# New step orders and PSUM bank assignments for a two-layer cross-attention kernel

## The reference

```python
# layer 0 (the image-token part is empty: 77 tokens, all text)
q, k, v = split(x @ Wq.T), split(text @ Wk.T), split(text @ Wv.T)
x = merge(softmax(q @ k.T / 4) @ v) @ Wo.T + bo + x
# layer 1
probs_t  = softmax(q @ k_t.T / 4)                 # 73 text tokens
text_out = probs_t @ v_t
qsem = l2norm(probs_t @ text_ehs)
fused = q @ k_ip.T / 4 + 0.5 * (qsem @ l2norm(ip_ehs).T)   # 4 image tokens
ip_out = (softmax(fused) * spatial_mask) @ v_ip
x = (text_out + ip_out) @ W_out + b_out + x
```

## Time and profile before

| what | value |
|---|---|
| median of 3 runs | 2372.46 us (2371.49 to 2372.55) |
| profiled execution: its own time / its span | 2372.11 us / 2370.3 us |
| mean granted TensorE clock | 0.984 of full speed, 1.00 from 430 us to 2290 us |
| busy share of the span: PE, DVE, ACT, POOL | 93%, 78%, 72%, 67% |
| DMA engines busy, first stage / second stage | 0.91 to 0.51 / about 0.44 |

### The profile page before, as it was taken

How to read it: one execution, slowest core, us unless ns; L and a number is a source line. 1 busy time by engine, 2 the same in 40 slices (tenths; PEclk the granted TensorE clock), 3 DMA queues, 4 the chain that set the end, 5 groups by cost and what they waited for, 6 DMA issues and landing times.

```text
span 2370.3 us, 86625 instructions
## 1 busy us (share of the span) xinstructions
PE 2200.8 (93%) x32824; PEld 1391.7 (59%) x32824; DVE 1849.0 (78%) x3709; ACT 1707.6 (72%) x2732; POOL 1589.4 (67%) x1056
## 2 busy tenths in 40 slices
PE   7999967999999999999999999999999999999984
PEld 5777744555555555555555555555555555555542
DVE  6856644888888888888888888888888888888873
ACT  4323326788888888888888888888888888888862
POOL 4121225777777777777777777777777777777762
PEclk9999988999999999999999999999999999999997
DMA  9877642444444444444444444444444444444431
GB/s 273 267 230 210 204 132 62 114 121 120 123 119 121 117 121 114 117 121 121 122 122 118 120 121 122 120 123 118 122 120 118 114 116 122 123 120 121 118 93 58
DMA packets 338308, 310.64 MB, mean 131 GB/s; under 512 B 180224, under 2 KB 281856, under 8 KB 337920
## 3 DMA queue, kind: packets, MB, share of 16 engines
q1 hardware_dynamic: 337920, 305.36, 46.1%
HBM read 164.66 MB, written 105.98 MB: 114 GB/s over the span
## 4 chain that ended last, share of the span: by engine, by line
PE 44%; POOL 14%; ACT 13%; issue 8%; DVE 3%; DMA 2%; SPq 1%; ACTq 0%; POOLq 0%; DVEq 0%
PE psum L1013 17%; ACT ef L1211 10%; POOL e L1445 7%; PE psum L1117 7%; PE psum L1099 5%; PE psum L1078 5%; POOL ust L1407 5%; PE psum L1016 3%; POOL al L1412 2%; ACT q_high L1192 2%; PE psum L1082 2%; PE psum L1037 2%; PE psum L1129 2%; DMA rb<-r_dram 1%; PE psum L1052 1%
## 5 line engine op out<-in xcount | busy, mean ns | idle before, releaser
L1445 POOL TENSOR_TENSOR e<-ef,eh 73x1024 f32<-73x1024 f32 x320 | 680.3, 2133 | 201.2 <-PE psum L1129 118.5
L1211 ACT ACTIVATE ef<-psum 73x1024 f32<-73x1024 f32 (+1 forms) x640 | 636.2, 1014 | 72.5 <-PE psum L1082 68.6
L1273 DVE TENSOR_REDUCE mneg<-psum 128x8 f16<-128x616 f32 (+3 forms) x512 | 450.9, 934 | 8.9 <-PE psum L1037 2.3
L1301 DVE TENSOR_TENSOR e<-psum,e 73x1024 f32<-73x1024 f32 x320 | 385.6, 1205 | 10.4 <-PE psum L1117 5.8
L1099 PE MATMUL psum<-ef,values 128*32 128x256 f32 x5120 | 360.1, 386 | 0.5
L1117 PE MATMUL psum<-eh,gram 128*73 128x512 f16 x1280 | 337.7, 386 | 18.7 <-DVE mneg L1273 14.2
L1226 ACT ACTIVATE eh<-ef 73x1024 f16<-73x1024 f32 x320 | 337.4, 1055 | 7.7 <-ACT ef L1211 0.4
L1219 ACT ACTIVATE ust<-psum 128x512 f32<-128x512 f32 x384 | 222.4, 596 | 124.0 <-POOL al L1412 116.2
L1407 POOL TENSOR_TENSOR ust<-ust,rb 128x768 f32<-128x768 f32 x128 | 232.3, 1815 | 104.9 <-DMA rb<-r_dram 104.9
L1412 POOL TENSOR_TENSOR al<-ust,ah 128x768 f16<-128x768 f32 x128 | 210.2, 1642 | 85.5 <-ACT ah L1251 85.5
L1281 DVE SCALAR_TENSOR_TENSOR q_low<-psum,q_high 128x512 f16<-128x512 f32 (+1 forms) x256 | 112.8, 481 | 182.4 <-ACT q_high L1192 182.4
(11 more groups left out here) (188 smaller groups left out, 4815.0 us busy)
## 6 DMA issues: line engine op xcount, KB each, us to landing
rb<-r_dram SPq DMA_DIRECT2D x128, 384.0 KB, 3.8
keys<-k_dram SPq DMA_DIRECT2D x128, 231.0 KB, 4.0
values<-v_dram SPq DMA_DIRECT2D x128, 192.5 KB
ust<-ust SPq DMA_DIRECT2D x512, 48.0 KB, 2.4
v_dram<-vst SPq DMA_DIRECT2D x64, 320.0 KB
out<-outt SPq DMA_DIRECT2D x64, 320.0 KB, 2.3
k_dram<-kst SPq DMA_DIRECT2D x32, 616.0 KB, 4.0
x<-in_x SPq DMA_DIRECT2D x32, 384.0 KB, 5.1
```

Source lines behind the costliest of these rows:

```text
L1211: act.activation(ef[l][0:m, unit_heads(n), :].rearrange("t h s -> t (h s)"), src, ACT.Exp, scale=SM).then_inc(s_exp[l], 1)
L1273: dve.tensor_reduce(dst, o, AX_X, ALU.max, negate=True).then_inc(s_max[l], 1)
L1301: dve.tensor_tensor(rest, banks(l, f"u{k}", 2)[0:m, :, :], rest, ALU.mult).then_inc(s_wr, 1)
L1445: pool.tensor_tensor(e2[0:m, k, :, :], ef[1][0:m, unit_heads(k), :], eh[0:m, unit_heads(k), :], ALU.subtract).then_inc(s_e2, 1)
```

## The change

All five lists of `ORDER` and the bank table `USES` are replaced. No step, no instruction and no transfer is added, removed or resized.

```diff
 ORDER = {
     "pe": """
-        1u2/3 1a1/3 0t1/1 1q0/2 1q1/2 0t2/1 0a0/1 1s0/2 0a1/1 1s1/2 0a2/1 1i/2 1a2/3 1u3/3 1m/2 1u4/3 1t0/2 0q0/0 0q1/0 1n0/3 1n1/3
-        1n2/3 1p/4 1u0/2 1n3/3 1n4/3 0s0/0 1a0/2 0s1/0 1u1/2 1t1/2 1o0/4 1o1/4 1t2/2 0m/0 1y/3 0o0/1 0o1/1 0t0/0""",
+        1q0/2 1q1/2 0t2/1 0a0/1 0a1/1 1s0/2 0a2/1 1s1/2 1u3/3 1a2/3 1i/2 1m/2 1u4/3 1t0/2 0q0/0 1n0/3 1p/4 1n1/3 1n2/3
+        1u0/2 0q1/0 0s0/0 1n3/3 1n4/3 0s1/0 1a0/2 1u1/2 1t1/2 1o0/4 1o1/4 1t2/2 0m/0 0o0/1 0o1/1 1y/3 0t0/0 1u2/2
+        1a1/2 0t1/0""",
     "act": """
-        0t0/1 0t1/1 1h4/3 1a1/3 0t2/1 1f/4 0t3/1 1q0/2 1q1/2 0t4/1 0a0/1 1r/3 0a1/1 0a2/1 1i/2 1a2/3 1m/2 0r/1 1t0/2 1h0/2
-        1t1/2 0q0/0 0q1/0 1h1/2 1g/4 1n/3 1a0/2 0g/1 1t2/2 1t3/2 1h2/2 1t4/2 0m/0 1h3/2""",
+        1f/4 0t2/1 0t3/1 1q0/2 1q1/2 0t4/1 0a0/1 0a1/1 0a2/1 1h4/3 1r/3 1a2/3 1m/2 1i/2 1t0/2 1h0/2 1t1/2 0q0/0 1h1/2
+        1g/4 0r/0 0q1/0 1n/3 1a0/2 0g/1 1t2/2 1t3/2 1h2/2 0m/0 1t4/2 1h3/2 0t0/0 0t1/0 1a1/2""",
     "dve": """
-        1y7/4 1y8/4 1y9/4 1y10/4 1y11/4 1w2/3 1y12/4 1y13/4 1y14/4 1y15/4 1y16/4 1y17/4 1y18/4 1ql0/2 1ql1/2 1tw0/2 1s0/2
-        1s1/2 1s2/2 1s3/2 1tw1/2 1w3/3 0d/1 1w4/3 0ql0/0 0ql1/0 1p/4 1w0/2 0s0/0 0s1/0 0s2/0 0s3/0 1w1/2 0tw0/0 1d/3 0tw1/0
-        1o0/4 1o1/4 1y0/3 1y1/3 1y2/3 1y3/3 1y4/3 1y5/3 1y6/3 0o0/1 0o1/1""",
+        1w2/3 1y15/4 1y16/4 1y17/4 1y18/4 1ql0/2 1tw0/2 1tw1/2 1ql1/2 1s0/2 1s1/2 1s2/2 1s3/2 1w3/3 0d/1 1w4/3 1p/4
+        0ql0/0 1w0/2 0s0/0 0s1/0 0s2/0 0ql1/0 0s3/0 1w1/2 1d/3 0tw0/0 1o0/4 0tw1/0 1o1/4 1y0/3 1y1/3 1y2/3 1y3/3 1y4/3
+        0o0/1 1y5/3 1y6/3 0o1/1 1y7/3 1y8/3 1y9/3 1y10/3 1y11/3 1y12/3 1y13/3 1y14/3""",
     "pool": """
-        1xh/2 1xl/2 1vb/4 1b3/3 0xh/0 1at/4 0xl/0 1b4/3 1c/2 1b0/2 1b1/2 1al/4 0at/1 0al/1 1b2/2 1kb/1""",
+        1b3/3 0xh/0 0xl/0 1b4/3 1at/4 1c/2 1b0/2 1b1/2 1al/4 0at/1 1vb/3 0al/1 1b2/2 1kb/1 1xh/1 1xl/1""",
     "sp": """
-        0x/0 1sh/4 1rl/4 1ps/4 1sl/3 0k/0 0ds/1 1v/2 1pl/4 1c/1 0rw/1 0sh/1 0rl/1 1ds/3 1g/1 1ns/3 1d/3 0v/0 1nl/3
-        1rw/3 1vi/2 1st/4 1ss/2 1k/1""",
+        0x/0 1k/2 1ps/4 0v/0 0ds/1 1pl/4 1v/2 0k/0 0rw/1 0sh/1 0rl/1 1ss/2 1vi/3 1ds/3 1ns/3 1d/3 1nl/3 1rw/3 1st/4
+        1sh/3 1g/1 1c/1 1rl/3 1sl/2""",
 }
 USES = [
-    "1a1 0a0 1s2 1u3 0q0 0s1 1u1 1t4",
-    "0t2 0t4 1s2 1u3 0q1 0s1 1u1 1t4 0t1",
-    "0t2 0t4 1s1 1i 1u4 1n 0s2 1t2 1t4 0t1",
-    "0t3 0t4 1s1 1a2 1u4 1u0 0s2 1t2 1t4 0t0",
-    "0t3 0t4 1s0 1s3 1t0 1u0 1t3 0m 0t0",
-    "1u2 1q0 1s0 1s3 1t0 1p 1a0 1t3 0o0",
-    "1u2 1q1 0a2 1t1 1p 0s0 0s3 1o0 0o1",
-    "0a1 1m 1t1 1p 0s0 0s3 1o1 1y",
+    "1q0 1s0 1s2 0q0 0s1 1u1 1t4 1a1",
+    "0t4 1s0 1s2 1m 1t0 0s1 1u1 1t4 0t1 0t2",
+    "0t4 1s1 1a2 1t0 1n 1a0 1t2 1t4 0t1 0t2",
+    "0t4 1s1 1u3 1t1 0q1 1t2 1t4 0t0 0t3",
+    "0t4 0a2 1u3 1t1 1u0 0s2 1t3 0t0 0t3",
+    "0a1 1s3 1u4 1p 1u0 0s2 1t3 0o0 1u2",
+    "1q1 1s3 1u4 1p 0s0 0s3 1o0 0m 0o1 1u2",
+    "0a0 1i 1p 0s0 0s3 1o1 1y",
 ]
```

## The result

The changed kernel takes 2415.1 us (median of 4 runs, 2410.45 to 2420.44) against 2372.51 us for the kernel before (4 runs, 2371.49 to 2374.67), a ratio of 1.0175 with a 95% interval of 1.0163 to 1.0187. Forecast were 2375.5 us and a range up to 2402, so the time lies outside it. The forecast itself stood for "no effect" (0.32). Of the three directions slower had the largest chance (0.46), the mechanism was rival 1 (0.18), and its size was taken too small.

The account below looks back on a forecast made before the run. No engine is full; a repeating cycle of 30.57 us, set by loops with PE's waits for banks, bounds it. Longest loop 30.58, taken as 30.62: +0.05 over 61 cycles, +3, giving 2375.5 us, range 2355 to 2402.

Parts of the forecast that it names:

- no effect: Whole kernel: the change only moves the waits and the cycle stays about the same, 2368 to 2377 us; chance 0.32.
- rival 1: Layer 1's keys land more than 5.0 us after issue and set the cycle: +0.35 per cycle, 2394 us; chance 0.18.
- Loop D: Loop through SP: sl waits for y12, then x and keys go out, land after 4.7, 1s0 follows; 30.3 us.
- B: Loop through ACT and POOL, by the exponential, h1 and b1 to 0o0 and the next 1q0: 30.58 us, the longest.
- A: Loop of PE with DVE, from 1q0 by 1s0, 1t0, 1u0 and 0o0 to the next 1q0: 30.54 us.
- C: Loop through the image softmax, where 0a0 waits for `pip`: 30.51 us.
- rival 3: Faster: two attend steps back to back on PE save more than 0.12; cycle 30.4, -0.17, 2362 us; chance 0.22.
- Rival 2: Slower: `pip`, w3 and h1 each come 0.05 to 0.1 later at engine handovers; cycle 30.72, 2382 us; chance 0.28.

Follow-up runs that it names:

- e1: Changed kernel with SP's load of layer 1's keys (1k) moved one step later, behind 1ps: 2517.04 us, ratio 1.0596.
- a2: Changed kernel with SP's 1k (layer 1's keys) ahead of 0x but still behind sl: 2377.61 us, ratio 1.0015.
- a1: Changed kernel with SP's 1k (layer 1's keys) moved ahead of 1sh, the sums' move, rl, sl and x: 2376.45 us, ratio 1.0010.
- d4: Changed kernel with the SP list of the kernel before, and in that list 1pl ahead of 1v: 2377.77 us, ratio 1.0013.
- d1: Changed kernel in all but SP's list, which is that of the kernel before: 2405.69 us, ratio 1.0139.
- d2: Kernel before in all but SP's list, which is that of the changed kernel: 2445.36 us, ratio 1.0305.
- c1: Changed kernel with 1k ahead of 1sh and PE's 1s0 ahead of 0a1: 2396.1 us, ratio 1.0095.
- g0: a1 with 0a1 in bank 4, 0a2 in bank 7, and PE's order 0a0 1s0 0a1 1s1 0a2 1a2 1u3: 2418.26 us, ratio 1.0191.
- g2: g0 with ACT's list changed to 1h4 1a2 1i 1m 1r 1t0 1h0 1t1: 2370.63 us, ratio 0.9985.

## Why the prediction was wrong, point by point

**Loop D, its sum and its slack of 0.3: the step that failed.** I had 30.3 for this loop, below B's 30.58, so the keys were to land in time. Its terms, as I had them and as the 58 cycles of the changed kernel from 490 to 2290 us have them in the mean:

| term | mine | measured, mean |
|---|---|---|
| keys sent for, from 1q0 | 0.05 before | 0.24 after (0.32 before to 1.22 after, median 0.17) |
| from there to landing | 4.7 | 4.86 (3.6 to 6.8, median 4.7) |
| landing to the start of 1s0 | nothing | 0.13 where 1s0 waits |
| 1s0 to the next 1q0 | 25.66 | 25.85 undisturbed, 26.08 with all |

These four differences are 0.29, 0.16, 0.13 and 0.19: loop D is 31.08 and not 30.3, half a microsecond above the other loops, and 1s0 waits in 42 of 58 cycles. So no single term was far off. The landing of 4.7 was even right in the median; what went wrong is that a slack of 0.3 was trusted to a sum in which every term was a little too small and one, the handover from the DMA to PE, was missing. The late issue comes in part from sl, whose issue took 0.32 to 1.45 (mean 0.56, median 0.54) where I had 0.44; x's took up to 0.87. My figure for the median, 4.0 from the earlier trace rows, was no bound on the good side: it holds layer 0's shorter loads.

By the Trainium skill, "DMA: Bandwidth & Descriptors", section "Queues, rings and completion order", a DMA engine consumes descriptors in ring order. The medians of 3.2 us in e1, 4.1 in a2 and 4.7 in the changed kernel agree with it, though no run here separates it from other ways of sharing the engines. The estimate of 2.5 us in the prediction rests on a formula that the Trainium skill, "DMA: Bandwidth & Descriptors", gives in its section "Anatomy of one DMA" for transfers issued by GpSimd, and these are issued by SP; the shortest load of layer 1's keys, in a1 and e1, took 2.6.

**What the spread costs.** From 1q0 to 1s0 the changed kernel takes 5.30 in the mean against 4.75: 58 x 0.55 = 31.8 us. The mean landing, 5.10, with its 0.13 gives 5.24 by itself, so the spread of issue and landing adds only 0.06 per cycle here. With that and the 0.23 between 25.85 and 26.08, the 31.08 become the measured mean cycle of 31.38. That spread costs anything at all is because PE keeps no slack from one cycle to the next: a cycle in which the keys are in time takes 30.60 to 30.87, not less, and one in which they are late takes more. The spread's larger price is the long waits, as follows.

**The rest, some 8 us: the clock.** From 1s0 to the next 1q0 the undisturbed 25.85 grew by 13.2 us in all over the stage, in a1 by 4.9. Six of the 57 cycles, behind waits of 1.00, 1.01, 1.09, 1.20, 1.62 and 3.33 us, took 27.15 to 28.15 for it, and carry 9.1 of the 13.2 us, which leaves about what a1 has; none of the others took more than 26.24, though two of them stood behind waits of 1.08 and 1.52. The granted clock is 0.91 or 0.95 in just these six cycles and 1.00 in the 51 others, and 1.00 in every cycle of a1 and of the kernel before. A cycle of each kind, the first with a wait of 1.62 us and the second with 0.76 (window, length, busy time by engine, granted clock, DMA share, GB/s):

```profile
929.00:962.62 33.62, 30.89 (x471) 18.54 (x467) 25.25 (x52) 25.20 (x39) 23.32 (x17) 0.95 0.37 107
962.62:994.04 31.42, 29.47 (x470) 18.01 (x466) 25.28 (x52) 25.25 (x40) 23.62 (x17) 1.00 0.44 123
```

Windows around that wait:

```profile
934.00:936.00 2.00, 0.55 (x13) 0.33 (x16) 0.13 (x1) 0.54 (x1) 1.03 (x2) 1.00 0.04 13
...
937.00:938.00 1.00, 0.70 (x6) 0.39 (x3) 1.00 (x2) 1.00 (x3) 0.43 (x1) 0.63 0.33 67
938.00:939.00 1.00, 1.00 (x4) 0.19 (x1) 1.00 (x2) 1.00 (x4) 0.81 (x1) 0.50 0.43 153
939.00:940.00 1.00, 1.00 (x9) 0.37 (x11) 0.87 (x2) 0.54 (x2) 1.00 (x1) 0.50 0.09 9
940.00:942.00 2.00, 2.00 (x26) 1.18 (x23) 1.07 (x2) 1.25 (x3) 2.00 (x2) 0.83 0.34 100
942.00:946.00 4.00, 4.00 (x62) 2.61 (x62) 1.30 (x2) 3.02 (x4) 1.14 (x3) 1.00 0.47 132
```

PE is busy 0.55 of 2.00 us; then, at work again, its granted clock is 0.50 (1.2 GHz) for over 2 us, and four matmuls of 1u that take 1.06 take 1.92. My sum had no term for this. e1 repeats it: 33 of the 54 cycles measured there have a granted clock of 0.90 to 0.95 and take 26.74 or more from 1s0 on, the 21 others have 1.00 and take 26.23 or less. Why a wait of 1.00 us is followed by the lower clock and one of 1.52 is not stays open. Just ahead of the longest wait SP's issues ran slower too (four of them 3.94 in place of 2.47).

**Loops A, B and C: right in the sum, by some luck in the terms.** In the 16 cycles without a wait for keys the changed kernel takes 30.60 to 30.87 (mine 30.62), and a1, all of it without such waits, has a median of 30.62. a1 ends 2.0 us above the kernel before as measured beside it (forecast +3), and d4 is at 2377.77. In detail:

- 1s0 starts 4.75 after 1q0 (mine 4.88). The two attend steps take 1.86 together in a1 and d4 and not 2.00. This is the saving of rival 3. It was not the maxima that took it back: 1s0 to 1t0 takes 5.17 in a1, as priced. From 1t0 to 1u0 it takes 4.84 (mine 4.70), since 1n0, 1p, 1n1 and 1n2 take 2.21 in the new order where 1n0, 1n1, 1n2 and 1p took 2.06, a cost that I had not priced; and from 1u0 to 0o0 9.40 (mine 9.35). The errors of -0.13 and +0.20 nearly cancel, which is luck.
- PE waits for the maxima behind 1s0 (cycle of the chain above, 0.38 and 0.30, and more on the weight loads), and 0s1 for DVE, 0.36:

```profile
1248.50 0.31 PE L1038 MATMUL psum<-keys,q_high 32*128 32x146 f16 x8 [0.38 <-DVE mneg L1274]
1249.17 1.06 PE L1118 MATMUL psum<-eh,gram 128*73 128x512 f16 x4 [0.30 <-DVE mneg L1274]
...
1260.49 0.32 PE L1038 MATMUL psum<-keys,q_high 32*128 32x154 f16 x8 [0.36 <-DVE mneg L1274]
```

- POOL no longer waits for `rb`: right, and worth nothing, as said. That POOL would wait for x instead (146.5 us in all) I had not seen; x, too, now goes out late, and only POOL's idle time covers it.
- Rival 2, handovers: no; a1's cycle of 30.57 leaves next to nothing for them.

**Size of rival 1.** I priced it at +0.35 per cycle from a landing of 5.3 to 5.5, and said that it decides once the keys land more than 5.0 after issue. Measured: +0.71, with a landing of 4.86 in the mean, because the other three terms had used up the slack, with the clock on top.

## What to carry to other kernels

A loop through a DMA that lies 0.3 us below the bound is not below it. Count it from the issue as its new place gives it, with the handover to the engine at the end, and read the landing from loads of the same place and company, not from a row that mixes two places. Here four small errors made 0.8 us and cost 1.75%, and one word of an order gave it back. Where lists of several engines and a bank table are set together, swapping in one of them tells little by itself (d1, d2, c1 and g0 all lost 1 to 3%); look at who waits then, move that one word, and measure again, as d4 and g2 did. And price an idle of a microsecond or more on TensorE above its length: behind six of eight such waits the cycle ran 1.3 to 2.3 us longer too.

## What the runs showed of the hardware

- A load of 231 KB landed 2.6 to 4.5 us after issue (median 3.2) when the 384 KB load of x ahead of it had been sent for 2.2 to 3.7 us before (e1, median 3.2), 2.8 to 5.6 (median 4.1) with the x load behind it (a2), and 3.6 to 6.8 (median 4.7) right behind the x load (changed kernel, layer 1).
- From the landing of the keys to the start of the matmuls that waited for them took 0.13 us in the mean of 42 cases.
- The issue of one and the same small load on SP takes 0.32 to 1.45 us (sl in the changed kernel, median 0.54), and all issues behind it shift by that.
- The granted clock of TensorE fell to 0.50 between 937 and 938 us, some 2 us after PE had taken up work again at 935.44 behind a wait of 1.62 us, and was back at 1.00 in the window from 942. It fell in 6 of 57 cycles of the changed kernel, behind waits of 1.00 to 3.33 us, and in 33 of 54 of e1.
- 24 matmuls of the norms in one piece, followed by 1p, took 2.06 us to the next step's start, and 2.21 with 1p behind the first 8 of them.
- Two attend steps back to back (32 matmuls) took 1.86 us, against 1.00 for one alone.
